# The set-up of a two-layer decoder kernel, with its clears, bias, relu and first scores moved

## The reference

```
x = x + attention(layernorm(x))       # 16 heads of 128; column sums of softmax(q k) weigh v, then w_o
# layer 0, cross attention ("linear"), per head h of 16, 64 features f:
k = heads(ctx @ Wk.T + bk)            # 16 wide
v = heads(ctx @ Wv.T + bv)
k_prime = relu(k @ Wkf.T) * mask      # 8 x 64 rows of context
kv = sum over rows of k_prime * v     # and k_sum, the same with v = 1
```

## Time and profile before

| | us |
|---|---|
| median of 3 runs (917.97, 919.81, 923.12) | 919.81 |
| the profiled execution, its own time | 922.4 |
| its span in the trace | 920.4 |
| VectorE, ScalarE, GpSimd busy | 720.4, 535.1, 368.4 |
| ctx, wk0, bk0: issued 3.28, 3.76, 4.27; to landing | 4.7, 4.8, 5.6 |
| X, tiles 4 to 7: issued 5.77; to landing | 7.8 |
| X, tiles 8 to 11: issued 10.37; to landing | 6.9 |
| bdk, keep0: issued 8.99, 9.90; to landing | 5.8, 6.0 |
| c_fc to landing | 6.2 |
| weight maxima of head 1, out, then gathered | 3.9, 3.3 |
| weight maxima of head 2, out (issued 91.96), then gathered | 1.5, 4.5 |
| statistics of four tiles, step to the next instruction | 1.86 |
| normalise (L699) and low half (L704): alone, step | 0.40, 0.42; 0.34 |
| scales (L661), then the small operations to L674 | 1.06, 0.80 |
| value bias (L690), 64x256; update of X (L931), 128x256 | 0.38; 0.48 |
| split_hi: two of L504, one of L507 | 0.90, 0.63 |
| ScalarE copies of 512 columns out of PSUM (L533; L528) | 0.60; 0.69 |
| v1's copies (L558) for one memory_values | 0.77 |
| exp of one step (L592, four of L596) | 2.45 |
| power (L459); weights_lo (L442); block maximum (L721) | 1.01; 1.18; 1.60 |
| the fp32 tensor_tensor 128x1024 of GpSimd (L1383) | 1.90 |
| key_values(0) and transpose 12, started | 33.37, 44.12 |

### The profile page before, as it was taken

How to read it: one execution, slowest core, us unless ns; L and a number is a source line. 1 busy time by engine, 2 the same in 40 slices (tenths; PEclk the granted TensorE clock), 3 DMA queues, 4 the chain that set the end, 5 groups by cost and what they waited for, 6 DMA issues and landing times. The chain is left out here.

```text
span 920.4 us, 18709 instructions
## 1 busy us (share of the span) xinstructions
PE 853.7 (93%) x6868; PEld 634.0 (69%) x6868; DVE 720.4 (78%) x1759; ACT 535.1 (58%) x1277; POOL 368.4 (40%) x354
## 2 busy tenths in 40 slices
PE   4788988999999999999999998999988889999786
PEld 3455766777777777777777776887855578787554
DVE  5748878878888788778887775897698779876885
ACT  1435576655665666556655744555566864545576
POOL 4103456545554455455555554043233031521410
PEclk9989999999999999999999998999999999999999
DMA  9123231011101110111000000000000010000001
GB/s 280 36 71 69 54 96 35 2 35 35 34 0 34 34 34 6 28 34 34 18 16 11 1 1 1 1 2 1 1 2 1 1 47 1 1 1 1 2 1 46
DMA packets 34722, 25.56 MB, mean 28 GB/s; under 512 B 9492, under 2 KB 31596, under 8 KB 34668
## 3 DMA queue, kind: packets, MB, share of 16 engines
q1 hardware_dynamic: 34380, 24.56, 10.3%
q10 hardware_dynamic: 288, 0.26, 0.1%
HBM read 22.65 MB, written 2.17 MB: 27 GB/s over the span
## 5 line engine op out<-in xcount | busy, mean ns | idle before, releaser
L483 POOL CAST exp_hi<-exp_scores 128x1024 f16<-128x1024 f32 x64 | 67.0, 1047 | 212.9 <-ACT exp_scores L596 212.9
L485 POOL TENSOR_TENSOR exp_lo<-exp_scores,exp_hi 128x1024 f16<-128x1024 f32 x64 | 140.7, 2199 | 5.1
L596 ACT ACTIVATE exp_scores<-banks,exp_bias,unscale 128x256 f32<-128x256 f32 x256 | 141.0, 560 | 2.1
L75 PE MATMUL banks<-value_out_hi,xn_t_hi 128*128 128x256 f16 x512 | 139.6, 273 | 0.3 <-DVE X L931 0.3
L76 PE MATMUL banks<-value_out_lo,xn_t_hi 128*128 128x256 f16 x512 | 139.6, 273 | 0.0
L77 PE MATMUL banks<-value_out_hi,xn_t_lo 128*128 128x256 f16 x512 | 139.6, 273 | 0.0
L1124 PE MATMUL banks<-qk 128*128 128x256 f32 x512 | 121.6, 380 | 9.0 <-ACT exp_scores L596 8.9
L1124 PEld LDWEIGHTS banks<-qk 128*128 128x128 f32 x512 | 96.6, 190 | 30.3 <-issue 9.6
L931 DVE SCALAR_TENSOR_TENSOR X<-banks,colsum,X 128x256 f32<-128x256 f32 x256 | 106.2, 477 | 11.0 <-DVE colsum L922 9.6
L575 ACT ACTIVATE qk<-banks 128x512 f32<-128x512 f32 x128 | 75.8, 601 | 57.9 <-PE banks L77 57.9
L906 DVE TENSOR_REDUCE neg_rowmax<-banks 128x4 f32<-128x1024 f32 x64 | 78.2, 1221 | 27.9 <-PE banks L1124 27.9
(11 more groups left out here) (253 smaller groups left out, 1973.9 us busy)
## 6 DMA issues: line engine op xcount, KB each, us to landing
head_weights<-in_wqkv_d SPq DMA_DIRECT2D x32, 128.0 KB, 3.7
weight_absmax_rows<-across_partitions SPq DMA_DIRECT2D x15, 256.0 KB, 4.0
X<-in_x_d SPq DMA_DIRECT2D x4, 512.0 KB, 7.3
head_weights<-in_wqkvt_d SPq DMA_DIRECT2D x16, 128.0 KB, 3.5
head_weights<-in_w_o_d SPq DMA_DIRECT2D x16, 128.0 KB, 3.5
out<-X SPq DMA_DIRECT2D x8, 256.0 KB, 2.1
ternary_then_kv_and_rows<-in_c_fc_d SPq DMA_DIRECT2D x1, 1024.0 KB, 6.2
ternary_then_kv_and_rows<-in_c_proj_d SPq DMA_DIRECT2D x1, 1024.0 KB, 8.0
```

The costliest lines, as they stand in the source:

```text
L75: nc.tensor.matmul(out, lhs[0], rhs[0], start=first, stop=False)
L483: nc.gpsimd.tensor_copy(probh[:, s1_.par], prob[:, s1_.par]).then_inc(exph_ready, 1)
L485: nc.gpsimd.tensor_tensor(probl[:, s1_.par], prob[:, s1_.par], probh[:, s1_.par], ALU.subtract).then_inc(expl_ready, 1)
L596: last = nc.scalar.activation(prob[:, s1_.par, t, :], sc_ps[t // ST][:, t % ST, :], ACT.Exp, bias=nbias[:, t:t + 1], scale=unscale[:, s1_. ...
```

## The change

- **Clears.** v1 is cleared after the first four normalisations instead of at once; kv0 after the powers of tiles 8 to 11. key_values(0) now waits for kv0's clear itself.
- **Value bias and mask.** GpSimd writes bias x mask and, in the 17th column, the mask into `vaug` (`kept_bias`). VectorE then computes psum x mask + that, per pair of batches, two pairs ahead of the token loop and two in it. The features are no longer masked. keep0's load moves from behind bdk to ahead of load_x(1).
- **relu** of the features moves from VectorE to ScalarE.
- **Statistics** of tiles 8 to 11 move ahead of the low halves of tiles 2 and 3; those of tiles 12 to 15 from t = 5 to t = 3. `block_max` moves from t = 4, 6, 8 to t = 8, 10, 12.
- **split_hi** of head 0 moves from t = 0, 2 to t = 5, 9.
- **First rows and scores.** TensorE runs the rows of step 0 ahead of key_values(2) and its scores ahead of memory_values(3) and key_values(3). ScalarE copies them inside its token loop, and copies the rows of step 1 after exp of step 0. The low half of head 0's M moves behind the row maximum in step 1, `block_sums` from step 0 to step 1, and TensorE's wait for kv_ready to step 2.
- TensorE's wait for k1_ready ahead of the token loop moves into memory_values.

```diff
@@ SP @@
         sp.dma_start(bv0[:, :], g.dram["bv0_d"].partition_broadcast(P)).then_inc(second_loads, 16)
+        sp.dma_start(keep0[:, :], g.dram["keep0_d"]).then_inc(second_loads, 16)
         load_x(1)
...
-        sp.dma_start(keep0[:, :], g.dram["keep0_d"]).then_inc(loads, 16)
@@ GpSimd @@
         rstd_of(0)
+        def kept_bias(a):
+            rows = slice(a * M, (a + 1) * M)
+            own = vaug[rows, :, a, :, 0:XD]
+            shape = [M, NP, XH, XD]
+            nc.gpsimd.tensor_tensor(own, bv0[rows, :].rearrange("p (h e) -> p h e", e=XD).unsqueeze(1).broadcast_to(shape),
+                                    keep0[rows, :].unsqueeze(2).unsqueeze(3).broadcast_to(shape),
+                                    ALU.mult).then_inc(bias_kept, 1)
+            pool.wait_ge(bias_kept, 2 * a + 1)
+            nc.gpsimd.tensor_copy(vaug[rows, :, a, :, XD:XD + 1],
+                                  keep0[rows, :].unsqueeze(2).unsqueeze(3).broadcast_to([M, NP, XH, 1])).then_inc(
+                                      bias_kept, 1)
+            pool.wait_ge(bias_kept, 2 * a + 2)
+        pool.wait_ge(xn_ready, TP)
         nc.gpsimd.memset(g.v1[:, :, :, :, :], 0.0).then_inc(cleared, 1)
+        pool.wait_ge(second_loads, 48)
+        pool.wait_ge(cleared, 3)
+        kept_bias(0)
+        rstd_of(1)
+        pool.wait_ge(rstd_ready, 2)
+        kept_bias(1)
+        rstd_of(2)
         nc.gpsimd.memset(g.kv0[:, :, :, :], 0.0).then_inc(cleared, 1)
-        for p in range(1, NP):
-            rstd_of(p)
+        rstd_of(3)
@@ ScalarE @@
+        def key_features(n):
+            act.wait_ge(kp_full, n + 1)
+            nc.scalar.activation(kp[:, n // KT, n % KT, :], bank[2 + n % 2], ACT.Relu).then_inc(kp_ready, 1)
+        def score_rows(i, par):
+            for s in range(2):
+                act.wait_ge(qk_full, i * 2 + s + 1)
+                nc.scalar.activation(qk[:, par, s, :], qk_ps[s], ACT.Copy).then_inc(qk_ready, 1)
-        for t in range(NT):
+        for t in range(NT - 2):
             if t + TP < NT:
                 token_half(t + TP)
+            if t == NT - TP:
+                key_features(6)
+                key_features(7)
+                score_rows(0, 0)
             if t % 4 == 0 and t > 0:
                 key_values(t // 4 - 1)
+            if t % 2 == 0 and t < NT - TP:
+                key_features(t // 2)
...
-            if t in (0, 2):
+            if t in (5, 9):
                 act.wait_ge(w_loaded[0], 64)
                 act.wait_ge(wscale_ready, 1)
-                split_hi(0, 0, t // 2)
+                split_hi(0, 0, t // 8)
...
+            if known(i) and i == 1:
+                score_rows(1, 1)
@@ VectorE @@
+        def context_values(p):
+            if p == 0:
+                dve.wait_ge(bias_kept, 4)
+                dve.wait_ge(v0_full, NP)
             for a in range(2):
                 rows = slice(a * M, (a + 1) * M)
-                nc.vector.memset(vaug[rows, :, a, :, XD:XD + 1], 1.0).then_inc(vaug_ready, 1)
-                for p in range(NP):
-                    nc.vector.tensor_tensor(vaug[rows, p, a, :, 0:XD],
...
+                own = vaug[rows, p, a, :, 0:XD]
+                nc.vector.scalar_tensor_tensor(out=own, in0=bank[4 + p // 2][rows, p % 2 * D:(p % 2 + 1) * D]
+                                               .rearrange("p (h e) -> p h e", e=XD), scalar=keep0[rows, p:p + 1], in1=own,
+                                               op0=ALU.mult, op1=ALU.add).then_inc(vaug_ready, 1)
...
         statistics(1)
+        statistics(2)
...
-        context_values()
+        context_values(0)
+        context_values(1)
         for t in range(NT):
-            if t in (1, 5):
-                statistics(2 + t // 4)
             if t + TP < NT:
                 xn_lo(t + TP)
             if t + TP + 2 < NT:
                 normalise(t + TP + 2)
-            if t % 2 == 0:
...
-                nc.vector.tensor_scalar(kp[:, n // KT, n % KT, :], bank[2 + n % 2], 0.0, keep0[:, n // KT:n // KT + 1],
-                                        ALU.max, ALU.mult).then_inc(kp_ready, 1)
-            if t in (4, 6, 8):
+            if t in (0, 1):
+                context_values(t + 2)
+            if t == 3:
+                statistics(3)
+            if t in (8, 10, 12):
                 dve.wait_ge(loads_n, 80)
-                block_max(t // 2 - 2)
+                block_max(t // 2 - 4)
...
@@ TensorE @@
-        pe.wait_ge(cleared, 4)
+        pe.wait_ge(cleared, 3)
         pe.wait_ge(k0_ready, KT)
-        pe.wait_ge(k1_ready, KT)
...
+        for t in range(NT - TP):
+            transpose_tokens(t + TP)
             if t % 4 == 0 and t > 0:
-                if t == 4:
-                    pe.wait_ge(vaug_ready, 2 * (NP + 1))
                 key_values(t // 4 - 1)
             if t % 2 == 0:
                 key_features(t // 2)
             if t % 4 == 1:
                 memory_values(t // 4)
+        key_features(6)
+        key_features(7)
+        pe.wait_ge(wlo_ready, 1)
+        pe.wait_ge(xnl_ready, NT)
+        score_rows(0, 0, slice(0, NPAIR))
+        key_values(2)
+        pe.wait_ge(kp_ready, 2 * NP)
+        pe.wait_ge(qk_ready, 2)
+        scores(0)
+        memory_values(3)
         key_values(NP - 1)
...
-        pe.wait_ge(xnl_ready, NT)
-        pe.wait_ge(kv_ready, NP)
```

More of the change, by code:

```diff
@@ L571, in step @@
             st = Step(i, c)
-            if runs(i, 0):
-                for s in range(2):
-                    act.wait_ge(qk_full, i * 2 + s + 1)
-                    nc.scalar.activation(qk[:, st.par, s, :], qk_ps[s], ACT.Copy).then_inc(qk_ready, 1)
+            if runs(i, 0) and not (known(i) and i <= 1):
+                score_rows(i, st.par)
             if later_head(i, c, 1):
@@ L1093, in _ @@
         value_out(0)
[L1094 to L1095 removed]
         def step(i, c, h, nth, r):
             st, s1_, s2 = Step(i, c), Step(i, c - 1), Step(i, c - 2)
[L1099 removed]
+            if runs(i, 0) and not (known(i) and i == 0):
                 if st.p == 0:
                     pe.wait_ge(wlo_ready, h * 2 + 1)
[L1103 to L1111 removed]
+                score_rows(i, st.u, slice(NPAIR * st.p, NPAIR * (st.p + 1)))
             if known(i) and i == LAST + 1:
@@ L1114, in step @@
                 gated_weights(1)
-            if runs(i, 1):
+            if runs(i, 1) and not (known(i) and i == 1):
                 pe.wait_ge(qk_ready, i * 2)
-                if not known(i) or i >= 2:
-                    pe.wait_ge(exp_ready, i - 1)
-                for b in range(2):
-                    for t in range(ST):
-                        q = slice(b * S + t * P, b * S + (t + 1) * P)
-                        kk = slice(b * S, (b + 1) * S)
-                        last = nc.tensor.matmul(sc_ps[b][:, t, :], qk[:, s1_.par, 0, q], qk[:, s1_.par, 1, kk],
-                                                start=True, stop=True)
-                last.then_inc(sc_full, 1)
+                pe.wait_ge(exp_ready, i - 1)
+                scores(s1_.par)
             if runs(i, 2):
+                if known(i) and i == 2:
+                    pe.wait_ge(kv_ready, NP)
                 if s2.p == 0:
```

57 lines of the change are left out of this document (28 added, 29 removed).

## The result

| | before | after |
|---|---|---|
| median of 20 executions each, us | 919.85 | 916.83 |
| lowest and highest | 917.97, 923.12 | 914.14, 921.35 |
| after / before, with its 95% interval | | 0.9963 [0.9952, 0.9974] |
| the profiled execution, its span | 922.4, 920.4 | 914.1, 912.3 |

The change makes the kernel 0.4% faster: 3.0 us by these medians, 8.3 were forecast. The 911.5 missed by 5.3 us; 916.83 lies inside the range, close to its upper end. The profiled execution, 914.1, is the fastest of the 20, so what its trace shows is not yet what the median got.

What follows compares the result with a forecast made beforehand. TensorE, 93% busy, sets the pace once heads run; VectorE decides the set-up. The head loop's first state product (the mark) comes 10.0 us earlier, 1.7 is given back: 8.3 off the median 919.8 gives 911.5, range 906.5 to 917.

Steps and rivals of the forecast that it cites:

- The walk: Set-up before the head loop: engine queues timed in code order put its first state product at 64.6 us at full clock.
- I take 0.38: VectorE's masked bias products before key_values(0): 0.38 us each; all eight at the upper end, 0.48, would cost 0.7 us.
- I take one stretch of 3.4 us: TensorE in the set-up: one half-clock stretch from 38.3, costing 1.7 us; none and two were the ends.
- the 7 that the prediction named as a sign of being wrong: Set-up between 25 and 60 us: half clock for over 7 us would show the prediction wrong.
- (a): Set-up and SP's queue: no half-clock stretch after the start, c_fc not holding the maxima; gain 11.7 us, 908.1; chance 0.2.
- What is given back: Start of the head loop: the second head's maxima, queued behind c_fc, delay step 2's exp; 1.7 us lost, range 0 to 3.
- scale_codes meets its data about as it is reached: Early head loop: scale_codes would find its data about when reached; no loss was counted for it.
- The head loop and the second part are the same code in both kernels: Everything from the head loop on: same code, so the question is how much earlier its first state product starts.
- (b): Set-up: ScalarE's queue becomes the bound, TensorE starves, the clock falls twice; gain 4 to 5 us, 915.3; chance 0.2.
- (c): Set-up: GpSimd's power blocks VectorE's normalisation; 1.1 us less gain, 912.6; chance 0.07.
- (d): GpSimd's masked bias products: slower by over half a per cent from 8.5 us each, 925.3 at 9; chance 0.03.
- (e): Set-up: tile 12, the last halves and exp(0) take the gains back in full; no difference, 919; chance 0.05.

Runs made afterwards that it cites:

- after_fed: The changed kernel with 52 idle matmuls put on TensorE where it waits; median 913.3 us, ratio 0.9921 to the kernel before.
- a_again: The changed kernel, unaltered, profiled a second time; median 916.58 us, ratio 0.9961 to the kernel before.
- before_fed: The kernel before with 49 idle matmuls put into TensorE's waits; median 917.46 us, ratio 0.9966 to the kernel before.
- fc_late: The changed kernel with the second head's weight maxima sent ahead of c_fc's load; median 916.68 us, ratio 0.9962 to the kernel before.
- a_third: The changed kernel, unaltered, for a third profile; one execution, 916.03 us.
- a_fourth: The changed kernel, unaltered, for a fourth profile; one execution, 916.38 us.
- fed_old_tail: after_fed with the old TensorE order behind the token loop and ScalarE's copies back in the steps; median 915.13 us, ratio 0.9939 to the kernel before.
- clears_only: The kernel before with only the clears of v1 and kv0 moved; median 918.83 us, ratio 0.9988 to the kernel before.
- clears_fed: before_fed with the clears of v1 and kv0 moved; median 917.31 us, ratio 0.9966 to the kernel before.
- fed_sums_first: after_fed with head 1's weight maxima and the NF4 sums and maxima sent ahead of c_fc's load; median 910.53 us, ratio 0.9895 to the kernel before.
- sums_first: The changed kernel with head 1's weight maxima and the NF4 sums and maxima sent ahead of c_fc's load; median 913.36 us, ratio 0.9917 to the kernel before.
- mask_in_relu: The changed kernel with the mask as relu's scale, the bias added on VectorE, no GpSimd products; median 917.26 us, ratio 0.9976 to the kernel before.
- fed_late_mask: after_fed with the edits of fc_late and mask_in_relu; median 912.96 us, ratio 0.9915 to the kernel before.
- fed_sums_mask: fed_sums_first with the edit of mask_in_relu; median 912.05 us, ratio 0.9906 to the kernel before.

## Why the prediction was right, and where it was wrong

The places were right and the sizes were not: 8.3 us were forecast, the profiles give 4.9 in the mean and the medians 3.0 to 4.0. The largest term that was mis-sized is the half clock on the changed side, 1.7 us for one stretch where 3.1 were measured in the mean; behind it stand 0.9 us of the head loop that were put at nothing, 0.7 of the masked bias and 0.4 of what is given back.

**The walk** was right in its kind: every stall that it named stood where it was said, on the engine that was said, and at full clock it gave 17.6 and 18.4 us for key_values(0) to first rows to mark, where after_fed has 17.60 and 18.45. relu, the bias products on GpSimd (1.89; said 1.9), normalise behind weights_lo and tile 12 came as walked.

**"I take 0.38"**, the masked bias on VectorE, was a term too small: 0.50 each (2.02 for four), above the 0.48 that was given as the upper end. key_values(0) came at 29.23 to 29.96, 28.6 walked. Of this 0.3 is the landing, on the mean of the four (third rows at 17.58 and not 17.3), and 0.7 lies behind it (12.02 instead of 11.3). This 0.7 is a net: from the first product to key_values(0) it was 6.50 instead of 5.25, of which eight products 0.12 longer make 1.0, and `scales` was done 0.5 earlier than walked.

**"I take one stretch of 3.4 us"** is the step that failed most. Its price was right (1.7 said, 1.6 measured), its count was not: in units of 3.4 us the four profiles have one, four, two and one, 1.6, 6.1, 2.9 and 1.6 us at the mark, 3.1 in the mean. a_again's 13.6 us are beyond the 7 that the prediction named as a sign of being wrong. I had reasoned from the gaps of one profile of the kernel before, whose other executions vary too, and had misread them: rival (a) sets the new gap of 2.85 against one of 4, but no gap of 4 us stands in that loop; the longest is 2.01, ahead of the transpose at 42.41, with one of 1.27 soon behind it. The wait before transpose 8, a second place for the fall, stood in my walk only as starts of transposes that I did not read as gaps. The mean mark of the changed kernel is 68.71 and of the old one 76.59: **7.9 us earlier, not 10.0**. The 2.0 us on the changed side are 1.4 clock, 0.7 products (net) and 0.3 landing, less the 0.3 that I had added for the walk, to 0.1. Held against before_fed the clock looks smaller: the old kernel pays 4.7 us for it (76.59 less 71.93), not 3.9, so it gives the change 1.6 us where I had 2.2. The other 1.6 of the miss at the mark are the full-clock walks, 6.3 apart instead of 7.85: 1.0 on the new side, 0.5 on the old one, whose mark is 71.93 and not 72.45.

**"What is given back", 1.7 us.** The place was right, the size in the mean 2.1 (2.0, 2.7, 1.9 and 1.6 between the mark and step 2). I had the weight maxima at 1.7; they cost 1.0 in after. The second half, "scale_codes meets its data about as it is reached", was wrong: it waits 2.96 us there, and that costs another 1.0. fc_late shows that the two are one wait in two places.

**"The head loop and the second part are the same code in both kernels"** hid 0.9 us. The lead falls by 0.34 behind step 17 and by 0.11 for every eight steps after, in after, a_again, a_third, a_fourth, and in all kernels with the changed token loop, fed_old_tail among them; in before_fed, clears_only and clears_fed it stands still. VectorE's update of X shows it. The groups of steps from 80 to 620 us; of before, then of after:
```profile
L931 DVE SCALAR_TENSOR_TENSOR X<-banks,colsum,X 128x256 f32<-128x256 f32 x256 | 106.2, 477 | 11.0 <-DVE colsum L922 9.6
```
```profile
L961 DVE SCALAR_TENSOR_TENSOR X<-banks,colsum,X 128x256 f32<-128x256 f32 x252 | 104.5, 478 | 12.8 <-DVE colsum L952 11.4
```
The time between colsum and the update, both VectorE's own, is 1.8 us more in total; it is 9.6 in all six profiles with the old token loop on VectorE and 11.4 in all twelve with the changed one, fed_old_tail among them. The excess stands at two steps of every eight, the length of the loop's body: 0.35 at each of the two the first time round, about 0.1 later. One such step, of before and of after:
```profile
202.14 1.66 DVE L931 SCALAR_TENSOR_TENSOR X<-banks,colsum,X 128x256 f32<-128x256 f32 x4 [0.20 <-DVE colsum L922]
```
```profile
203.87 1.66 DVE L961 SCALAR_TENSOR_TENSOR X<-banks,colsum,X 128x256 f32<-128x256 f32 x4 [0.55 <-DVE colsum L952]
```
No data and no other engine ends it. TensorE's program was changed in before_fed and GpSimd's in clears_only, without effect; those of VectorE, ScalarE and SP are changed in every kernel that shows it. Which of them does it, and how, stays open: no kernel was made for that alone.

**The sum** with what was measured: 7.9 - 2.1 - 0.9 = 4.9 us, and the mean span of the four profiles (915.15) lies 4.9 below that of the three (920.07). That it closes so well is in part luck, with seven profiles and two terms of 0.2 to 0.3 us left out (the stretch near 145 and the time behind the head loop) that cancel. The medians say 3.0 in the first comparison and, over all executions of this study, 4.0 (920.75 of 113; 916.8 of 32). The last us between the means and the medians isn't accounted for execution by execution, since only profiled ones can be read; the draw of the clock is wide enough for it: the changed kernel's executions range from 0.986 to 0.994 in mean clock, the old one's from 0.988 to 0.993. A further stretch near 141 to 152 us, which costs 1.65, comes and goes in both kernels alike.

**The rivals.** (b) holds in half of it: the clock does fall more than once in some executions, but behind VectorE's normalised tiles, not ScalarE's halves. The gain is what it gave, 4 to 5, by the mean of the profiles; since its cause was another, that is luck. (a) did not come: all four profiles of the changed kernel have at least one stretch, and c_fc held the maxima in them. fed_sums_first, which takes both out by hand, has a median of 910.5 where (a) gave 908.1. (c) fell: the power (19.33 to 20.44) and a normalisation of 0.40 at 19.34 ran side by side. The Trainium skill's rule in "SBUF — State Buffer", section "Who interferes with whom", is contradicted by that row as by the earlier trace rows. (d) fell: 1.89 us each. (e) fell by the interval, which ends at 0.9974.

## What to carry to other kernels

The walk of the queues gave the full-clock times to 1 us; the clock of a stage full of stalls gave nothing so firm. Price such a stage by several executions, or by its waits, each as a place where the clock may fall, and set the range by the draw; idle matmuls in those waits were worth 3.5 us in the median here. An engine that is given less to do comes earlier to its next instruction: see what that then meets, as kv0's clear met a normalisation. On an in-order queue send the small transfers that an engine waits for ahead of the large load that nobody waits for, all of them, since one moved alone hands its wait to the next. And a loop that is copied unchanged can still run differently behind a changed program: compare a step far down, not only the first.

## What the runs showed of the hardware

- The same program ran from 3.4 to 13.6 us at half clock in the same 45 us. The stretches began at 39.0, at 30.3 and 40.5, at 38.6 and at 31.7, behind waits of TensorE of 1.24 to 2.38 us. The Trainium skill, "TensorE: Matmul & The Clock Gate", section "What's actually happening", says that the monitor's window runs on by itself and is not set back by a kernel's start, so that the change of clock moves from run to run. These starts agree in that they move; that the same wait is followed by half clock in one execution and not in another is what the traces add. The mean clock of a kernel therefore isn't a property of its code alone.
- 52 idle matmuls took the stretches away in the profiled execution and brought the executions to a clock of 0.994 to 0.996, where the kernel without them had 0.986 to 0.994.
- The landing of the third 512 KB of X moved by 1.7 us between executions of one order of loads (16.66 in fc_late to 18.38 in fed_sums_first). From 17.21 to 18.38 key_values(0) moved with it, one for one within 0.2 us, in the kernels with the products on GpSimd; with the two earlier landings it did not come earlier (30.10 in fc_late, 29.92 in sums_first).
- A GpSimd product of 64 rows x 1024 with both inputs broadcast costs 1.89 us, as much as the 1.90 of the plain one of 128 rows x 1024.
- A clear on GpSimd (kv0, 1.91 us) stretched a normalisation on VectorE from 0.40 to 2.20 us in mask_in_relu, fed_late_mask and fed_sums_mask, though neither waits for the other; the power (1.01 us, from 19.42 in mask_in_relu) left one at 0.40.
- Two VectorE instructions in a row of the head loop, code unchanged, stand 0.55 us apart instead of 0.20 at two steps, and about 0.3 at the same places of later rounds of the loop, in every profile of the changed program; cause open.
